# Edge chunks at the border of two destination tiles: one multiplication with a half-and-half one-hot, in a graph network on one Trainium2 core

## What is computed

```
agg = segment_sum(w[:, None] * x[src], dst, num_segments=6250)   # w is 1 in the first networks
L0: h = relu(mean_agg(x) @ W1l.T + b1l + x @ W1r.T); mean_agg(h) @ W2l.T + b2l + h @ W2r.T
L1: relu(gcn(x, W_conv, b_conv)) @ W_lin + b_lin                 # gcn: norm * agg of x @ W, with self-loops
L2: gcn(relu(gcn(x, W1, b1)), W2, b2)
L3: three layers: h = relu(layernorm(h + sum_k hop_k(h) @ W[l, k] + bias)), k = 0..3
    hop_k = segment_sum(w * hop_(k-1)[src], dst), w with edge_weight
x = layernorm(x + L_i(x)) after each network
```

## Time and profile before

| | us |
|---|---|
| median of 3 runs | 7355.84 (7343.09 to 7356.77) |
| the profiled execution, as a time | 7354.22 |
| its span, first to last instruction | 7352.4 |
| TensorE busy | 6796.8 (92%) |
| GpSimd busy | 4721.4 (64%) |
| VectorE busy | 2161.7 (29%) |
| mean DMA rate | 283 GB/s |

### The profile page before, as it was taken

How to read it: one execution, slowest core, us unless ns; L and a number is a source line. 1 busy time by engine, 2 the same in 40 slices (tenths; PEclk the granted TensorE clock), 3 DMA queues, 4 the chain that set the end, 5 groups by cost and what they waited for, 6 DMA issues and landing times.

```text
span 7352.4 us, 75993 instructions
## 1 busy us (share of the span) xinstructions
PE 6796.8 (92%) x25725; PEld 4000.4 (54%) x25726; DVE 2161.7 (29%) x8178; ACT 363.9 (5%) x1003; POOL 4721.4 (64%) x4931
## 2 busy tenths in 40 slices
PE   0699749999999999998999999999999999999999
PEld 0598325555555555555555555555555555555555
DVE  8444602222222111222222233222222332222244
ACT  0000000000010000000000000000000000000000
POOL 0677777677666776776647477464765747557474
PEclk9999879999999999999999999999999999999999
DMA  9877737788787887887878788787888878788887
GB/s 367 348 290 295 251 129 263 253 295 275 279 279 266 285 295 275 307 273 278 291 275 297 272 315 297 274 288 271 299 300 281 298 279 291 271 291 301 296 298 246
DMA packets 606900, 2083.26 MB, mean 283 GB/s; under 512 B 133012, under 2 KB 332599, under 8 KB 411580
## 3 DMA queue, kind: packets, MB, share of 16 engines
q1 hardware_dynamic: 332302, 1667.02, 63.2%
q0 software_dynamic: 157840, 242.67, 10.9%
q10 hardware_dynamic: 116412, 169.16, 6.3%
HBM read 1804.71 MB, written 274.95 MB: 283 GB/s over the span
## 4 chain that ended last, share of the span: by engine, by line
PE 71%; DMA 11%; issue 10%; POOL 7%; DVE 0%; SPq 0%; ACT 0%; POOLq 0%; ACTq 0%; DVEq 0%
PE pwide L1021 57%; PE pstep L1051 11%; POOL counts L591 4%; DMA counts<-lane_val,lane_idx 4%; DMA counts<-zz 2%; POOL ring_f L628 2%; PE pwide L1105 1%; DMA weights<-lane_val,lane_idx 1%; POOL weights L591 1%; DMA ring_f<-table,f_src 1%; DMA room<-weights 1%; DMA ring_f<-in_x,f_src 1%; PE pwide L1104 0%; PE pwide L1067 0%; PE pwide L1071 0%
## 5 line engine op out<-in xcount | busy, mean ns | idle before, releaser
L628 POOL DMA_INDIRECT ring_f<-table,f_src x3456 | 3287.4, 951 | 1915.5 <-issue 874.9
L1021 PE MATMUL pwide<-room,hcur 128*128 128x512 f32 (+1 forms) x6468 | 2696.6, 561 | 116.2 <-DMA room<-counts 109.3
L1021 PE MATMUL pwide<-room,acc 128*128 128x512 f32 (+1 forms) x6370 | 2654.9, 560 | 25.2 <-DMA room<-weights 23.3
L1021 PEld LDWEIGHTS pwide<-room,hcur 128*128 128x128 f32 x6468 | 1127.7, 191 | 1167.5 <-issue 1162.1
L1021 PEld LDWEIGHTS pwide<-room,acc 128*128 128x128 f32 x6370 | 1106.2, 191 | 1040.6 <-issue 1037.4
L1051 PEld LDWEIGHTS pstep<-hot,ring_f 128*128 128x128 f32 x7956 | 1092.4, 192 | 649.3 <-issue 556.1
L1537 DVE TENSOR_SCALAR hot<-iota,f_dst,f_wgt 128x128 f32<-128x128 f32 x2808 | 793.0, 361 | 1588.0 <-PE pstep L1051 1575.1
L1051 PE MATMUL pstep<-hot,ring_f 128*128 128x128 f32 x7956 | 1126.7, 277 | 85.4 <-DMA ring_f<-table,f_src 68.2
L591 POOL DMA_INDIRECT counts<-lane_val,lane_idx x660 | 648.4, 982 | 222.7 <-issue 180.5
L591 POOL DMA_INDIRECT weights<-lane_val,lane_idx x568 | 557.2, 981 | 173.1 <-issue 162.1
L1536 DVE TENSOR_SCALAR hot<-iota,f_dst 128x128 f32<-128x128 f32 x1170 | 261.8, 303 | 812.3 <-PE pstep L1051 798.6
(11 more groups left out here) (261 smaller groups left out, 1686.4 us busy)
## 6 DMA issues: line engine op xcount, KB each, us to landing
room<-weights SPq DMA_DIRECT2D x864, 1024.0 KB
room<-counts SPq DMA_DIRECT2D x540, 1024.0 KB
counts<-zz ACTq DMA_DIRECT2D x64, 1792.0 KB
weights<-zz SPq DMA_DIRECT2D x57, 1792.0 KB
ring_f<-table,f_src POOLq DMA_INDIRECT x3456
room<-weights SPq DMA_DIRECT2D x180, 256.0 KB
room<-counts SPq DMA_DIRECT2D x105, 256.0 KB
table<-acc ACTq DMA_DIRECT2D x84, 256.0 KB
```

Of the source, the lines that this page charges most:

```text
L628: pool.indirect_dma_start(out=ring_f[:, slot, :], out_offset=None, in_=rows_from[:, :], in_offset=bass.IndirectOffsetOnAxis(ap=f_src[:, c: ...
L1021: ins = pe.matmul(bank[:, 0:w * P], x_of(a)[:, first + o, :], room[:, n % SLOTS, o * w * P:(o + 1) * w * P], start=begins, stop=ends and n ...
```

## The change

The border chunks 16 to 18 of a pair are multiplied once, with a one-hot that covers nodes 64 to 191 of the pair's 256 nodes, that is the second half of the first tile and the first half of the second; the output goes to the 128 PSUM columns that span both halves. `STP` becomes 36, with 12 batches to a pair. So that both tiles' columns have been written before a matmul spans them, the chunks are taken in another order (`TAKEN`): chunk 19 goes before 16, 17 and 18. The index row `iota` is 192 long, and a border one-hot compares with its columns 64 to 191. The half-spanning one-hot is right only if the chunks 16 to 18 hold no edge outside nodes 64 to 191, so the set-up counts the edges below two more nodes of each of 8 pairs (64 and 192), and tests them: 64 border counts in all (`NB`) in place of 48. The general path and the degree count use the first 128 columns of `iota` as before.

```
-STP = 39
+STP = 36
-def last_step(c):
-    return c if c < MIX else 2 * c - MIX + 1 if c < MIX + 3 else c + 3
-def step_of(i):
-    if i < MIX:
-        return i, 0, True
-    if i < MIX + 6:
-        return MIX + (i - MIX) // 2, (i - MIX) % 2, (i - MIX) % 2 == 0
-    return i - 3, 1, True
+TAKEN = list(range(MIX)) + [MIX + 3, MIX, MIX + 1, MIX + 2] + list(range(MIX + 4, CHP))
+def column_of(c):
+    return 0 if c < MIX else P // 2 if c < MIX + 3 else P
...
+NODES = [n * P for n in range(1, TILES)] + [2 * p * P + n for p in range(MOST) for n in (P // 2, 3 * P // 2)]
+NB = len(NODES)
+BOUNDS = [(max(0, 17 * n - 1500) // (P * P), min((17 * n + 1500) // (P * P), CG - 1)) for n in NODES]
...
 # gpsimd, gathers
+                        at = pair * CHP + TAKEN[slot]
                         if PAIR0[a] + pair > 0:
-                            freed = (PAIR0[a] + pair - 1) * STP + last_step(slot)
+                            freed = (PAIR0[a] + pair - 1) * STP + slot
...
-                                                in_offset=bass.IndirectOffsetOnAxis(ap=f_src[:, c:c + 1], axis=0)
+                                                in_offset=bass.IndirectOffsetOnAxis(ap=f_src[:, at:at + 1], axis=0)
...
 # tensor, edges
-                j = 2 * pair + side - first
+                to = (2 * pair - first) * P + column_of(TAKEN[c])
...
-                if fresh:
-                    pe.wait_ge(chunk_in[c], (PAIR0[a] + pair + 1) * 16)
+                pe.wait_ge(chunk_in[c], (PAIR0[a] + pair + 1) * 16)
-                ins = pe.matmul(bank[:, j * P:(j + 1) * P], row, one, start=begins, stop=ends and not own)
+                ins = pe.matmul(bank[:, to:to + P], row, one, start=begins, stop=ends and not own)
...
 # vector, set-up
-            for n0 in range(0, NS, 6):
-                some = range(n0, min(n0 + 6, NS))
+            for n0 in range(0, NB, 6):
+                some = range(n0, min(n0 + 6, NB))
...
+            low, high = (begun[0:1, at:at + 2 * MOST - 1:2] for at in (NS + 1, NS + 2))
+            for row, edge, op, least in ((3, low, ALU.is_le, MIX), (4, high, ALU.is_ge, MIX + 3)):
+                link(V.tensor_tensor(fits[:, row, 0:MOST], edge, begun[0:1, 0:2 * MOST:2], ALU.subtract))
+                link(V.tensor_scalar(fits[:, row, 0:MOST], fits[:, row, 0:MOST], float(least * P), None, op))
+                link(V.tensor_tensor(fits[:, 2, 0:MOST], fits[:, 2, 0:MOST], fits[:, row, 0:MOST], ALU.mult))
...
 # vector, one_hot
+                side, at = (1, 0) if from0 == P else (0, from0)
+                col, to, numbers = c - WALK * side, hot[:, (BATCH0[a] * HB + s) % HOTS, :], iota[:, at:at + P]
-                    return V.tensor_scalar(to, iota[:, :], f_dst[:, 2 * pair + side, col:col + 1], None, ALU.is_equal)
+                    return V.tensor_scalar(to, numbers, f_dst[:, 2 * pair + side, col:col + 1], None, ALU.is_equal)
```

More of the change, by code:

```diff
@@ L57 @@
 FH = 5
[L58 removed]
+assert STP % HB == 0 and HOTS % HB == 0 and 2 * MIX + 4 == CHP == STP
 KINDS = [0, 1, 2, 3, 4] + ["hop1", "hop2", "hop3"] * LAYERS
[L62 to L71 removed]
+TAKEN = list(range(MIX)) + [MIX + 3, MIX, MIX + 1, MIX + 2] + list(range(MIX + 4, CHP))
+def column_of(c):
+    return 0 if c < MIX else P // 2 if c < MIX + 3 else P
 class Split:
@@ L151, with alike @@
 EDGES = E + 66 * P
-BOUNDS = [(max(0, 17 * P * n - 1500) // (P * P), min((17 * P * n + 1500) // (P * P), CG - 1)) for n in range(1, TILES)]
+NODES = [n * P for n in range(1, TILES)] + [2 * p * P + n for p in range(MOST) for n in (P // 2, 3 * P // 2)]
+NB = len(NODES)
+BOUNDS = [(max(0, 17 * n - 1500) // (P * P), min((17 * n + 1500) // (P * P), CG - 1)) for n in NODES]
+def alike(key):
+    for k, run in itertools.groupby(range(NB), key):
+        run = list(run)
+        yield k, run[0], run[-1] + 1
 SPAN = CHP - WALK
@@ L160, in pace @@
     p, (pair, slot) = SPLITS[a], divmod(c, CHP)
-    first = slot if slot < MIX else MIX + 2 * (slot - MIX) if slot < MIX + 3 else slot + 3
-    m = p.beat_of((pair * STP + first) // HB) * p.mm // p.beats
+    m = p.beat_of((pair * STP + slot) // HB) * p.mm // p.beats
     k, m = divmod(m, 4 * TILES)
@@ L251, in program @@
         f_dst_flat = f_dst[:, :, :].rearrange("p t c -> p (t c)")
-        begun = sb("begun", [P, NS + 1])
-        from_ = sb("from_", [P, NS + 1])
-        over = sb("over", [1, 2, NS])
+        begun = sb("begun", [P, NB + 1])
+        from_ = sb("from_", [P, NB + 1])
+        over = sb("over", [1, 2, NB])
         fits = sb("fits", [1, 5, PAIRS])
@@ L871, in _ @@
             pe.wait_ge(v_begun, 1)
-            pe.matmul(pstep[1][:, 2:3 + NS], ones[:, :], begun[:, :], start=True, stop=True)
+            pe.matmul(pstep[1][:, 2:3 + NB], ones[:, :], begun[:, :], start=True, stop=True)
             pe.wait_ge(v_same, 2)
@@ L1034, in edges @@
             def edges(a, p, batch, n):
-                pair, i = divmod(batch * HB + n, STP)
-                c, side, fresh = step_of(i)
+                pair, c = divmod(batch * HB + n, STP)
                 q = p.group(pair)
                 first, w, at = sum(p.sparse[:q]), p.sparse[q], SPARSE_AT[a, q]
-                j = 2 * pair + side - first
+                to = (2 * pair - first) * P + column_of(TAKEN[c])
                 bank = pstep[at % 2]
-                begins, ends = 2 * pair == first and i == 0, 2 * pair + 2 == first + w and i == STP - 1
+                begins, ends = 2 * pair == first and c == 0, 2 * pair + 2 == first + w and c == STP - 1
                 own = KINDS[a] in (2, 3, 4)
@@ L1262, in _ @@
             V.memset(from_[:, 0:1], 0.0)
[L1263 to L1269, removed]
+            for lo, at, end in alike(lambda n: BOUNDS[n][0]):
+                V.memset(from_[:, at + 1:end + 1], float(lo * P * P))
+            for size, at, end in alike(lambda n: BOUNDS[n][1] - BOUNDS[n][0] + 1):
+                link(V.memset(over[:, 0, at:end], float(size * P * P) - 0.5))
             dve.wait_ge(in_edges, 48)
             link(V.tensor_copy(dnat, dnat_i))
-            for n0 in range(0, NS, 6):
-                some = range(n0, min(n0 + 6, NS))
+            for n0 in range(0, NB, 6):
+                some = range(n0, min(n0 + 6, NB))
                 for i, n in enumerate(some):
@@ L1288, in _ @@
             dve.wait_ge(p_flag, 1)
-            link(V.tensor_tensor(over[:, 0, :], over[:, 0, :], pstep[1][0:1, 3:3 + NS], ALU.is_ge))
+            link(V.tensor_tensor(over[:, 0, :], over[:, 0, :], pstep[1][0:1, 3:3 + NB], ALU.is_ge))
             link(V.reduce_sum(fit[:, 0:1], over[:, 0, :], axis=mybir.AxisListType.X))
-            link(V.tensor_scalar(over[:, 1, :], pstep[1][0:1, 3:3 + NS], 0.5, None, ALU.is_ge))
+            link(V.tensor_scalar(over[:, 1, :], pstep[1][0:1, 3:3 + NB], 0.5, None, ALU.is_ge))
             link(V.reduce_sum(fit[:, 1:2], over[:, 1, :], axis=mybir.AxisListType.X))
-            link(V.tensor_tensor(begun[:, :], pstep[1][:, 2:3 + NS], from_[:, :], ALU.add))
+            link(V.tensor_tensor(begun[:, :], pstep[1][:, 2:3 + NB], from_[:, :], ALU.add))
             full = PAIRS - 1
@@ L1329, in _ @@
                 link(V.tensor_tensor(flag[:, 0:1], flag[:, 0:1], flag[:, 1:2], ALU.mult))
-            for col, least in ((0, NS), (1, NS), (2, PAIRS)):
+            for col, least in ((0, NB), (1, NB), (2, PAIRS)):
                 link(V.tensor_scalar(flag[:, 1:2], fit[:, col:col + 1], least - 0.5, None, ALU.is_ge))
@@ L1531, in one_hot @@
             def one_hot(a, s):
-                pair, i = divmod(s, STP)
-                c, side, _ = step_of(i)
-                col, to = c - WALK * side, hot[:, (BATCH0[a] * HB + s) % HOTS, :]
+                pair, slot = divmod(s, STP)
+                c = TAKEN[slot]
+                from0 = column_of(c)
+                side, at = (1, 0) if from0 == P else (0, from0)
+                col, to, numbers = c - WALK * side, hot[:, (BATCH0[a] * HB + s) % HOTS, :], iota[:, at:at + P]
                 if a < STAGES:
-                    return V.tensor_scalar(to, iota[:, :], f_dst[:, 2 * pair + side, col:col + 1], None, ALU.is_equal)
-                return V.tensor_scalar(to, iota[:, :], f_dst[:, 2 * pair + side, col:col + 1], f_wgt[:, pair * CHP + c:pair * CHP + c + 1],
+                    return V.tensor_scalar(to, numbers, f_dst[:, 2 * pair + side, col:col + 1], None, ALU.is_equal)
+                return V.tensor_scalar(to, numbers, f_dst[:, 2 * pair + side, col:col + 1], f_wgt[:, pair * CHP + c:pair * CHP + c + 1],
                                        ALU.is_equal, ALU.mult)
```

14 lines of the change are left out of this document (7 added, 7 removed).

## The result

| | before | after |
|---|---|---|
| median | 7355.08 | 7287.97 (4 runs, 7281.92 to 7300.0) |
| ratio, 95% interval | 1 | 0.991 (0.9896 to 0.9924) |
| the profiled execution, as a time | 7354.22 | 7300.0 |
| its span | 7352.4 | 7298.1 |
| stages 1 to 4, first gather to first gather | 1951.3 | 1930.1 |

The change saves 67 us by the medians. Two single runs further down, one of before at 8420.3 us and one of `pe_back2` at 9029.53, were slow at a lower granted clock (0.80 and 0.78) and are left out of the ratios.

What follows compares the result with a forecast made beforehand. Set-up was taken as bound by VectorE, scatter and stage 0 by GpSimd, thirteen stages by TensorE. Span 7352.4 - 64.3 + 5.6 = 7293.7, or 7295.5 as a time; adjusted to before's median, 7297, range 7283 to 7318.

Steps and rivals of the forecast that it cites:

- the side given 0.90: Whole kernel: faster by more than about 0.2% (15 us), given a chance of 0.90.
- The three terms: Removed TensorE passes in stages 1 to 13, -64.3 us; added set-up, +5.6; stage 0, counted at nothing.
- Rival 3: Stage 0 gives its 4.0 us, set-up costs 1.2, waits at stage starts shrink: about 7286 us; chance 0.11.
- The removed passes: Stages 1 to 13 on TensorE: 96 pairs each lose a batch of 0.67 us, 64.3 us less.
- Stage 0: GpSimd's gathers pace it, so 4.0 us less on TensorE counts at nothing; bound 0 to 4.0 us gained.
- The set-up: VectorE ahead of the flag: 16 more node counts, memsets and six tests, less a hidden wait, add 5.6 us.
- After it VectorE sat idle 2.53 us for a load, which hides that much: Set-up on VectorE: the idle wait after the counts hides 2.5 of 6.9 us added, leaving 4.4.
- Rival 1: GpSimd becomes the bound in stages 1 to 4: saving 48.2 us, time 7313; chance 0.09.
- the spare time: GpSimd at the ends of stages 1 to 4: 17 to 27 us, smallest 13.2, falling to 9 to 23.
- Rival 2: DMA really bounds the late stages: 48.2 us turn into waits, only 16.1 kept, time 7345; chance 0.06.
- Rival 4: Border matmuls of stages 1 to 13: output over two tiles costs more than an aligned one, hence 7480; chance 0.02.
- rival 5: New graph test fails and all engines take the general path, over 14,500 us; chance 0.01 with similar surprises.

Runs made afterwards that it cites:

- `pe_back2`: Changed kernel with each border chunk multiplied a second time into the same columns, border edges counting double; 7349.99 us, ratio 0.9991.
- `again`: The changed kernel once more with no edit, for a second profile and more times; 7292.26 us, ratio 0.9914.
- `steps_only`: Changed kernel with the set-up counting and testing only the 48 tile borders as before; 7296.53 us, ratio 0.9918.
- `stage0_only2`: Changed kernel with 36 steps to a pair in stage 0 alone and 39 elsewhere, second try; 7364.54 us, ratio 1.0012.
- `zero_later`: Changed kernel with ScalarE's zero-fills of the dense matrix held until the edge lists have landed; 7287.45 us, ratio 0.9908.
- `setup_only`: Changed kernel with all 39 old steps to a pair in the old order, so only the set-up is changed; 7358.63 us, ratio 1.0005.
- `late_only2`: Changed kernel with 36 steps to a pair in stages 5 to 13 alone and 39 elsewhere, second try; 7305.01 us, ratio 0.9932.
- `stage0_only`: Changed kernel with 36 steps in stage 0 alone, first try on a chip where before took 9018.76 us; 9079.73 us, ratio 1.0065.
- `late_only`: Changed kernel with 36 steps in stages 5 to 13 alone, first try on a chip where before took 9018.76 us; 9044.62 us, ratio 1.0021.

## Why the prediction was right, and where it was off

The forecast of 7297 us is 9 above the median of after and 5 above that of `again`; both lie in the range and on the side given 0.90. Against the profiled execution, where the sum said 7295.5, it was 7300.0. The three terms were off by -4.9, +2.9 and +6.4 us, so part of the nearness is luck, errors that cancel. Rival 3's time, 7286, lies nearer to the median of after than the forecast does, though two of its three reasons did not come true.

**The removed passes, -64.3 forecast.** Right in mechanism and a little small. In the profiled pair TensorE's busy time in stages 1 to 13 fell by 62.8 us and the length by 69.2; over all kernels it is 70.2. The term is short by 5.9 us: I had priced a removed batch at its passes alone, and left shorter waits to rival 3. By the means of the table 4.1 us of them are shorter waits, and one is plain: TensorE's wait for the first block of `weights` at the start of stage 5 was 12.6 us and became 8.9, and is 8.7 to 9.0 in every kernel of that table with 12 batches to a pair in stages 1 to 4, 12.1 to 12.8 in those with 13. By the Trainium skill ("TensorE: Matmul & The Clock Gate", Back-to-back issue gap) the passes would have been worth an estimated 46.7 us; `pe_back2` shows 62.3 us of work for them and 0.11 us a pass in the starts, so the f32 row was the better guide here.

**Stage 0, nothing forecast, bound 0 to 4.0 gained.** This is one of two steps that failed, by its sign. GpSimd paces the stage as said: first to last gather took 269.4 us, against 268.8. But TensorE, with less to do, waits more at the end. TensorE's timeline of after:

```profile
1362.10 1.22 PE L1055 MATMUL pstep<-hot,ring_f 128*128 128x128 f32 x4 [2.04 <-DMA ring_f<-in_x,f_src]
1363.12 3.78 PE L1027 MATMUL pwide<-room,hcur 128*128 128x128 f32 x22
...
1372.76 5.30 PE L1027 MATMUL pwide<-room,hcur 128*128 128x128 f32 x46
1382.47 4.51 PE L1027 MATMUL pwide<-room,acc 128*128 128x512 f32 x6 [4.42 <-DMA room<-counts]
```

and of before:

```profile
1353.33 2.62 PE L1021 MATMUL pwide<-room,hcur 128*128 128x128 f32 x22
...
1361.80 5.30 PE L1021 MATMUL pwide<-room,hcur 128*128 128x128 f32 x46
1368.48 2.81 PE L1021 MATMUL pwide<-room,acc 128*128 128x512 f32 x6 [1.38 <-DMA room<-counts]
```

The 22 passes took 3.78 us and not 2.62, the six wide ones 4.51 and not 2.81: the granted clock of 1350 to 1368 was 0.91 and of 1368 to 1390 0.92, where before had 1.00 in both, so TensorE had fallen to 1.2 GHz for a part of them. Counted from stage 0's last gather, the 46 passes began 1.8 us later than in before, the wait for the matrix was 3.0 us longer and the six wide passes 1.7, so that ScalarE issued the stage's last table write 6.6 us later (36.7 us behind that gather, against 30.1). The write then took 5.2 us and not 6.0 until it ended GpSimd's wait, and the idle time ahead of stage 1 grew by 5.8.

The other kernels with 36 steps in stage 0 waited 2.6 to 4.7 us for the matrix, those with 39 steps 1.4. The slow passes are in `again`, `steps_only` and `stage0_only2` as well. `zero_later` waited 3.14 us, but its passes took 2.62 and 2.81 us, and its idle time is 36.4. `pe_back2`, where TensorE has its old work, is nearly back: its 22 passes take 2.62 us, but the six wide ones are slow there too:

```profile
1377.32 4.51 PE L1027 MATMUL pwide<-room,acc 128*128 128x512 f32 x6 [1.87 <-DMA room<-counts]
```

Its last table write comes 2.5 us later than in before, and a quicker landing, 3.4 us, hides that in its 35.01 us. So a longer idle time goes with fewer steps in stage 0 (36.4 to 42.0 us against 34.7 to 35.2 in the table, and 42.04 in `stage0_only2`, which has them there alone), and the slow passes, 2.9 us, are the larger part of the 4.5 us between `after` and `zero_later`. What makes the clock fall in one and not in the other, and why the matrix is waited for 1 to 3 us longer, was not tried.

**The set-up, +5.6 forecast.** The added instructions cost what I said: 7.4 us of counts against 6.9, 1.2 of tests, and 5.9 at the flag where the load is early. The other step that failed is "After it VectorE sat idle 2.53 us for a load, which hides that much": it took the load's landing as fixed. In the profiled executions it moved by 9.6 us, and the flag by 10.8. GpSimd made up some of it over its 660 scatters, which took 868.6 us and not 871.1. They are not quite back to back, as I had them: one scatter of before, at 238.66, waits 11.54 us for an earlier one to land, and the same one of after 10.91. By the medians the set-up's cost is small: `setup_only` is 3.5 us over before.

**The rivals.** Rival 1, GpSimd as the bound in stages 1 to 4, fell: the spare time at their ends grew to 18.9, 23.2, 15.4 and 27.5 us where I had expected 9 to 23 (the gathers of 1887 to 3338, against the earlier trace rows). I had taken 4.0 us a stage off the spare time, though I had written myself that GpSimd's last gathers wait for batches that come earlier too. They did: GpSimd's waits for TensorE's edge and dense matmuls before a gather fell from 77.5 to 50.7 us over the four stages. I also had the spare time as 17 to 27 us where the earlier trace rows have 13.22 at the end of stage 3; the argument used the 13.2. Rival 2, DMA as the bound, fell: the late stage has a DMA share of 0.85 against 0.84, and 432 of 435 us busy on TensorE, and `late_only2` had its stages 5 to 13 54 us shorter than before. (The "79 to 85%" in this rival are 78 to 84% in the earlier trace rows.) The rule that I had cited for it from the Trainium skill ("Perfetto Trace Analysis", Identifying the Most-Contended Engine) would have read the 54% of weight loads as slack; the trace disagrees, since removing 62.8 us of busy time brought 69.2. Rival 4 fell by the rows of `pe_back2`, rival 5 by the counts of instructions. Rival 3 described the gain in the stages rightly and was wrong on stage 0 and on the set-up.

## What to carry to other kernels

In stages where the busiest engine's instructions start without gaps, count the removed ones at their start-to-start step; here that gave 64 of 70 us. Where another engine paces a stage, less work for the first is not free of effect: here TensorE waited longer at the stage's end, its clock fell for a while in four of the five profiles with fewer steps there, and the next stage started 1 to 7 us late. And an idle gap before a load covers added work only if the load itself stays put; look at what it competes with first.

## What the hardware showed that I had not expected

A list load of 20.2 KB took 56 to 65 us to issue on SP beside the zero-fills, and 5.4 us when they were held back. Its time differed by up to 8.5 us between programs whose work at that point is alike.

TensorE's granted clock fell to 1.2 GHz for parts of two stretches in which it waited 2.0 and 4.4 us: six wide passes took 4.51 us in place of 2.81. It did not fall in `zero_later`, which waited 3.14 us at the same place.

The same program took 7355 us on one chip and 9019 on another. A profile there (`stage0_only`) has the DMA at 16 GB/s for 800 us ahead of stage 0, and `late_only`, with 48.5 us saved in the late stages, still took 26 us more than before.
